# A wavelet block with attention on Trainium2: VectorE's order in the head, and where the last image's maps and attention layers stand

## The reference

```python
ll, lh, hl, hh = haar_dwt(x)                                  # 80 x 80 each
fused = relu(bn(conv1x1(concat(ll, lh, hl, hh), fusion_w)))   # 1024 -> 256 channels
sp_map = conv7x7(concat(mean_c(fused), max_c(fused)), sa_w)   # 2 -> 1 channel, 80 x 80
s = sigmoid(sp_map) * fused
ch = sigmoid(mlp(mean_hw(s)) + mlp(max_hw(s)))                # 256 -> 16 -> 256
proj = relu(bn(conv1x1(ch * s, proj_w)))                      # 256 -> 1024 channels
return haar_idwt(proj) + x
```

## Time and profile before

| | us |
|---|---|
| median of three runs | 2400.68 (2397.55 to 2400.82) |
| the profiled execution | 2394.07 |
| its span, first to last instruction | 2392.3 |

### The profile page before, as it was taken

One profiled execution on the slowest core, in us unless ns is written; L12 is line 12 of the kernel. 1 busy time (PEld: TensorE's weight loads), 2 busy tenths in 40 slices (PEclk: granted clock), 3 DMA queues, 4 the chain that ended last, 5 costly groups with the idle time before them and its releaser, 6 DMA issues. The chain is left out here.

```text
span 2392.3 us, 30200 instructions
## 1 busy us (share of the span) xinstructions
PE 2303.3 (96%) x11109; PEld 2039.9 (85%) x11109; DVE 2065.7 (86%) x2571; ACT 1137.2 (48%) x1535; POOL 584.9 (24%) x549
## 2 busy tenths in 40 slices
PE   7998799999999999999999999999999999998897
PEld 6886689888898988989899898988889898886786
DVE  6885688898888988899888989889888898889899
ACT  4443544465444554455444564446544464434433
POOL 0110122122221221211222112212212112133698
PEclk9999899999999999999999999999999999999999
DMA  5454499999999999999999999999999999989998
GB/s 188 168 183 147 151 277 283 278 310 284 294 286 295 288 286 288 288 281 306 282 277 297 293 307 281 283 278 297 295 293 283 283 307 280 280 238 286 346 354 324
DMA packets 112759, 660.54 MB, mean 276 GB/s; under 512 B 17698, under 2 KB 18788, under 8 KB 112356
## 3 DMA queue, kind: packets, MB, share of 16 engines
q1 hardware_dynamic: 84964, 479.04, 51.8%
q0 software_dynamic: 27648, 179.58, 39.2%
HBM read 448.24 MB, written 210.33 MB: 275 GB/s over the span
## 5 line engine op out<-in xcount | busy, mean ns | idle before, releaser
L542 PE MATMUL pp<-y_hi,wp_hi 128*128 128x480 f32 (+1 forms) x1792 | 670.5, 374 | 24.8 <-DVE sd L863 11.7
L633 ACT ACTIVATE x_hi<-xin 128x1920 fp32r<-128x1920 f32 (+1 forms) x224 | 418.7, 1869 | 542.9 <-PE pfs L570 461.0
L542 PE MATMUL pp<-y_lo,wp_hi 128*128 128x480 f32 (+1 forms) x1792 | 666.1, 372 | 0.0
L542 PE MATMUL pp<-y_hi,wp_lo 128*128 128x480 f32 (+1 forms) x1792 | 664.1, 371 | 0.0
L777 DVE TENSOR_TENSOR x_lo<-xin,x_hi 128x1920 fp32r<-128x1920 f32 (+1 forms) x224 | 461.5, 2060 | 214.1 <-ACT x_hi L633 213.1
L570 PE MATMUL pfs<-x_hi,wf_hi 128*128 128x480 f32 (+1 forms) x1648 | 616.4, 374 | 13.7 <-DVE x_lo L777 13.3
L570 PE MATMUL pfs<-x_lo,wf_hi 128*128 128x480 f32 (+1 forms) x1648 | 614.3, 373 | 0.0
L570 PE MATMUL pfs<-x_hi,wf_lo 128*128 128x480 f32 (+1 forms) x1648 | 614.2, 373 | 0.0
L666 ACT ACTIVATE relu<-pp,t 128x480 f32<-128x480 f32 (+1 forms) x448 | 285.6, 639 | 351.6 <-PE pp L542 351.2
L880 DVE SCALAR_TENSOR_TENSOR xre<-sd,both 128x960 f32<-128x960 f32 (+1 forms) x364 | 410.2, 1169 | 6.1
L542 PEld LDWEIGHTS pp<-y_hi,wp_hi 128*128 128x128 f32 x1792 | 338.2, 189 | 76.0 <-DVE sd L863 15.5
(11 more groups left out here) (105 smaller groups left out, 1595.5 us busy)
## 6 DMA issues: line engine op xcount, KB each, us to landing
xin<-in_x_dram SPq DMA_DIRECT2D x160, 960.0 KB, 7.8
out_dram<-xre SPq DMA_DIRECT2D x160, 960.0 KB, 7.5
xre<-in_x_dram POOLq DMA_DIRECT2D x136, 960.0 KB, 10.3
xin<-in_x_dram SPq DMA_DIRECT2D x64, 800.0 KB, 7.3
out_dram<-xre SPq DMA_DIRECT2D x63, 800.0 KB, 5.9
xre<-in_x_dram POOLq DMA_DIRECT2D x56, 800.0 KB, 9.5
xre<-in_x_dram SPq DMA_DIRECT2D x24, 960.0 KB, 7.0
sigb<-sig_scratch SPq DMA_DIRECT2D x28, 400.0 KB, 8.5
```

The lines of the kernel that those rows point to most:

```text
L542: mm = pe.matmul(pp[j][:, 0:n_px], w[:, kt, cols], y[:, s.pc, kt, 0:n_px], start=(kt == 0 and m == 0), stop=(kt == CT - 1 and m == 2))
L633: nc.scalar.activation(halves(x_hi, i, k), pairs(i, k), ACT.Copy).then_inc(xhi_ready[i], 1)
```

## The change

Four orders change, and no arithmetic.

- Head, VectorE (`head_body`, slots 0 to 20): `turn` comes first, then `x_lower` of the first half, then `pool_chunks`, both `gate`s, `spatial_maps`, `bands`, then `x_lower` of the second half. `turn` now stands ahead of the `x_lower` pair of its slot.
- Head, GpSimd: `channel_sum` no longer waits for the first half of `x_lo` of the next tile.
- Slot 112: TensorE's `gather` of the maps moves behind both halves of the projection, `spatial_maps` on VectorE behind the second `cells`, and `store_maps` on SyncE behind `store(s.kc, 0)` and `load_residual(s.kn, 1)`.
- Slot 118: the first attention layer stands between the banks LL and HH of the projection's second half, the second between HH and HL; ScalarE's relu of it stands ahead of the relu of HH; VectorE's `lower` of the next tile stands between the second `butterflies` and `cells` (before: at the top of slot 119).

```diff
             def body(s):
...
+                if s.phase == 0 and s.a:
+                    store_maps(s)
...
                 if s.c:
                     store(s.kc, 0)
                 if s.c_next and not adding(s.kn, 1):
                     load_residual(s.kn, 1)
+                if s.phase == 0 and not s.a:
+                    store_maps(s)
...
                 gp.wait_ge(f_ready, CT * (k + 1))
-                if s.load_next:
+                if s.load_next and s.c:
                     gp.wait_ge(xlo_ready[0], s.k + 2)
...
                 for n, j in enumerate((LH, LL, HH, HL)):
+                    if s.phase == LAST - 1 and not s.a and i == 1:
+                        if n == 2:
+                            squeeze_channels(s)
+                        if n == 3:
+                            excite_channels(s)
...
-                if s.phase == LAST and not s.a:
-                    excite_channels(s)
...
                 if s.c:
                     project(s, 1)
+                if s.phase == 0 and not s.a:
+                    gather(s)
...
                 for n, j in enumerate((LH, HH)):
+                    if n == 1 and i == 1 and s.phase == LAST - 1 and not s.a:
+                        hidden(s)
...
+            def head_body(s):
+
+                if s.turn:
+                    turn(s)
+                x_lower(s.k + 1, 0)
+                if s.phase == LAST - 1:
+                    pool_chunks(s)
+                if s.phase in GATED:
+                    for hand in range(2):
+                        gate(s, GATED[s.phase][hand])
+                if s.phase == 0:
+                    spatial_maps(s)
+                bands(s)
+                x_lower(s.k + 1, 1)
+                if s.c_next:
+                    lower(s.kn)
...
             def body(s):
-                ahead = s.phase == LAST
+                if not s.c:
+                    head_body(s)
+                    return
...
                 butterflies(s, 1)
+                if s.phase == LAST - 1 and not s.a:
+                    lower(s.kn)
                 cells(s, 1)
+                if s.phase == 0 and not s.a:
+                    spatial_maps(s)
```

More of the change, by code:

```diff
@@ L366, in load_sig, with store_maps @@
                              ).then_inc(sigb_landed[c % 2], 16)
+            def store_maps(s):
+                sp.wait_ge(across_ready, 2 * (s.nb + 1))
+                for m in range(2):
+                    sp.dma_start(map_dram[m:m + 1, :].rearrange("o (h p j) -> (o p) h j", h=2, j=GROUP),
+                                 across_all[:, m, :, :]).then_inc(map_stored, 16)
             def store_sig(s):
@@ L585, in convolve, with gather, squeeze_channels @@
                 mm.then_inc(conv_psum, 1)
+            def gather(s):
+                pe.wait_ge(mlp_ready, 2)
+                pe.wait_ge(blockmax_ready, s.k)
+                pe.wait_ge(blocksum_ready, s.k)
+                for to, blocks in ((across_sum, blocksum), (across, blockmax)):
+                    for h in range(2):
+                        n = NPX // GROUP // 2
+                        mm = pe.transpose(to[:, h * P:(h + 1) * P], blocks[:, h * n:(h + 1) * n], ident[:, :])
+                mm.then_inc(across_psum, 1)
+            def squeeze_channels(s):
+                pe.wait_ge(pool_ready, 2 * (s.nb + 1))
+                for i in range(CT):
+                    mm = pe.matmul(squeezed, squeeze[:, i, :], pool[:, i, :], start=(i == 0), stop=(i == CT - 1))
+                mm.then_inc(hid_psum, 1)
             def body(s):
@@ L614, in body @@
                     project(s, 1)
+                if s.phase == 0 and not s.a:
+                    gather(s)
                 if s.phase == 1 and not s.a:
                     convolve(s)
[L617 to L621, removed]
+                if s.phase == LAST - 1 and s.a:
+                    squeeze_channels(s)
             body(slots[0])
@@ L694, in upper, with hidden @@
                                          scale=ch[:, i:i + 1]).then_inc(hi_ready, 1)
+            def hidden(s):
+                act.wait_ge(hid_psum, s.nb + 1)
+                nc.scalar.activation(hid[:, :], squeezed, ACT.Relu, accum_out=hid_sum[:, :]).then_inc(hid_ready, 1)
             def body(s):
-                if s.phase == LAST:
-                    act.wait_ge(hid_psum, s.nb + 1)
-                    nc.scalar.activation(hid[:, :], squeezed, ACT.Relu, accum_out=hid_sum[:, :]).then_inc(hid_ready, 1)
+                if s.phase == LAST and s.a:
+                    hidden(s)
                 if s.phase == LAST:
@@ L950, in pool_chunks @@
                 nc.vector.tensor_reduce(pool[:, :, 1], part[:, 1, :, :], AX.X, ALU.max).then_inc(pool_ready, 1)
+            def head_body(s):
[13 more added lines that the diff above has]
+                    lower(s.kn)
             def body(s):
-                ahead = s.phase == LAST
+                if not s.c:
+                    head_body(s)
+                    return
                 if s.load_next:
                     x_lower(s.k + 1, 0)
[L956 to L966, removed]
+                butterflies(s, 0)
+                if s.phase == 0:
+                    turn(s)
+                if s.phase == LAST - 1:
+                    pool_chunks(s)
+                cells(s, 0)
                 if s.c_next and not s.next_is_first:
                     lower(s.kn)
-                if s.phase == LAST - 1 and not s.c:
-                    pool_chunks(s)
-                if s.turn and not (s.phase == 0 and s.c):
+                if s.turn and s.phase != 0:
                     turn(s)
@@ L974, in body @@
                     gate(s, GATED[s.phase][0])
-                if s.load_next and other(s.k) == other(s.k + 1):
+                if s.load_next:
                     x_lower(s.k + 1, 1)
-                if s.phase == 0:
+                if s.phase == 0 and s.a:
                     spatial_maps(s)
@@ L980, in body @@
                     lower(s.kn)
[L981 to L984, removed]
+                butterflies(s, 1)
+                if s.phase == LAST - 1 and not s.a:
+                    lower(s.kn)
+                cells(s, 1)
+                if s.phase == 0 and not s.a:
+                    spatial_maps(s)
                 if s.phase in GATED:
```

## The result

The change took 33.7 us off the median: 2365.39 us (2359.91 to 2370.51, four runs) against 2399.11 for the kernel before on the same chip, a ratio of 0.9861 with an interval of 0.9835 to 0.9887. Two more comparisons of the same file gave 0.9888 (0.9873 to 0.9902) and 0.9865 (0.9844 to 0.9887). The profiled execution took 2366.2 us, with a span of 2364.4; the prediction had 2368.6 for that and 2375 for the median. It was right in direction and in range, and 9.6 us high.

The account below looks back on a forecast made before the run. VectorE's order was taken to hold up TensorE in the head, engines other than TensorE to bind the tail. Head -28, slot 112 +2.5, slot 118 0 sum to -25.5: 2368.6 profiled, 2375 median after carrying over 6.6; range 2364 to 2387.

Parts of the forecast that it names:

- slots 1 to 13: Head: the new VectorE order leaves 3.5 of TensorE's 7.6 us idle; gain 4, bounds 7 and a loss of 6.
- slots 14 and 15: Head: TensorE's 7.1 us wait for blockmax goes, and 1 us of slow clock with it; gain 8.
- slots 16 to 20: Head: VectorE becomes the bound at 12 us a long slot against TensorE's 10.7; gain 13.5, bounds 9 and 17.
- slot 21: End of the head: runs at full clock without a long idle ahead of it; gain 2.5.
- the exclusion: Head: GpSimd's sum and a two-input VectorE instruction can't overlap; 1.0 us charged per turn, about 5 us more gain without it.
- The wait for the broadcast: Slot 16: gate 0's broadcast lands at 11.1 us after the convolution's end, where VectorE would come at 9.7.
- Tail, slot 112: Map stores queue behind three transfers, so the convolution starts 1.7 us later; loss 2.5, bounds -1 (a gain) and 5.
- a convolution that starts earlier relative to the middle's end: Tail: sign that the forecast is wrong and the tail gains.
- the 2147 less the head's gain: Tail, slot 112: sign that the forecast is right, SyncE's map stores issued after this time.
- Tail, slot 118: TensorE starts slot 119 2 us earlier, but GpSimd's adding waits for a residual's DMA; 0, bounds gain 2.5, loss 1.
- (2): Rival: the tail pays as TensorE's waits suggest, 5.3 us for the gather and 2 for the gate; 2365, chance 0.1.
- (3) to (5): Rivals: port and DMA cost double in head, 2390, chance 0.11; slower turns, 2411, 0.02; no effect, 2400, 0.03.

Follow-up runs that it names:

- sum_small: The full change with GpSimd's channel sum in slots 1 to 20 cut to 8 columns; ratio 0.9839 to the kernel before, 2358.4 us.
- gate_only: The kernel before with the change of slot 118 alone; ratio 1.0001 (0.9992 to 1.0010).
- maps_only: The kernel before with the change of slot 112 alone; ratio 1.0005 (0.9993 to 1.0017).
- head_order: The full change, but outside slots 14 and 15 turn stands behind bands or gates and GpSimd's sum waits for x_lo again; ratio 0.9870 to the kernel before.

## Why the prediction was right, and where its sizes were off

By slot starts in the two traces, the terms of the head:

```
                     before   after   gain   forecast
slots 1 to 13        139.5    134.1    5.4     4
slots 14 and 15       32.1     23.8    8.3     8
slots 16 to 20        72.1     56.8   15.3    13.5
slot 21*              13.7     11.3    2.3     2.5
to its projection    289.7    258.1   31.5    28
```

(*: to its projection. The last row is counted from the span's start, the terms from slot 1.)

**Slots 1 to 13.** The mechanism was as told: the sum meets `x_lo`, `turn` pays 1.0 us, TensorE's waits stay under 1 us (three, 0.74 to 0.85, all at a tile of 400 columns or behind one). The longer ones, up to 1.7, are in slots 17 to 20. The remaining idle was 2.5 us by the window, where 3.5 was reckoned. The sentence that without the exclusion the head would gain 5 us more had the size too small and the place half wrong: `sum_small` shows 6.6, of which only 2.8 here and 4.0 in slots 16 to 20, where VectorE is the bound and the sum's microsecond had been reckoned in the slot's 12.0 without being called a cost of the exclusion.

**Slots 14 and 15** came out as forecast, with no idle before the gather.

**Slots 16 to 20.** Slots 17 to 20 take 12.2, 11.4, 11.2 and 11.5 us. The wait for the broadcast that was forecast as new is 0.83 us:

```profile
200.54 0.99 DVE L918 CUSTOM_DVE_ANT_0 fused<-fused,sigb 128x800 f32<-128x800 f32 x1 [0.83 <-DMA sigb<-sig_scratch]
```

It was reckoned at 1.4 (11.1 less 9.7). Slots 17 to 19 cost VectorE's sum, 34.8 us for the 34.6 reckoned (12.0 and twice 11.3). Two things made the gain larger than forecast. The 1 us taken off for shared DMA engines wasn't paid, and the last step, `turn` and the first `x_lo` of slot 20, took 4.9 us instead of 6.1: the sum met the `x_lo` ahead of it, and the maximum took 0.56. The bounds, 9 and 17, held it.

**Tail, slot 112.** Right in mechanism: SyncE's order and not TensorE sets the convolution, the map load falls from 4.9 to 1.7 us, the stores behind the transfers cost more than that, and TensorE idles 5.2 to 10 us (8 to 9 forecast) and then runs at the lower clock. Two signs named beforehand were misleading: a convolution that starts earlier relative to the middle's end was to show a gain, and in the first trace it did start 2 us earlier, through one quicker DMA; for the same reason the maps' stores were issued at 2112.80, some 3 us before the 2147 less the head's gain that was to show the forecast right. Over seven traces the edit is at +1.8 to +2.3 us. What of this reaches the end isn't settled; the time is 1.2 us with an interval from -1.7 to 4.1.

**Tail, slot 118.** Zero was right and for the reason given: `gate_only` is 1.0001, and GpSimd's run still begins on a DMA, behind a wait of 6.5 us. TensorE's start of slot 119 comes 1.3 us earlier, where 2 was reckoned: it is 7.4 us behind TensorE's last wait for `sd` in `gate_only` and 8.7 in `before`.

**The sum.** The profiled execution missed by 2.4 us (2366.2 for 2368.6). The other 7.2 us of the median's miss come of the step that carried over 6.6 us from one profiled execution to the median: after's own profiled execution lies 0.8 *above* its median. Before's trace was a quick one: from the last fusion to the end it took 271.8 us, the least of all seven in the table, whose others take 274.0 to 281.5. Between medians the gain is 33.7, 27.0 (2397.1 less 2370.1) and 30.3 us (2398.9 less 2368.6) in three comparisons, around the 31.5 of the head, against a forecast sum of 25.5.

**The rivals.** (2), the tail paying 7.3 us as TensorE's waits suggest, gives 2365, which is the time measured, but by chance, and it is wrong all the same: `maps_only` and `gate_only` exclude 7.3. (3) to (5) are out by the time.

## What to carry to other kernels

When an engine with slack is late, look at the order of its queue before its work: moving what nobody waits for into the gap ahead of an input that isn't ready took 31 us out of a head of 290 without removing an instruction. An idle engine in a stretch where another (here VectorE, GpSimd and the DMA engines) sets the end is no sum to be gained; four edits there moved waits from one place to another and nothing at the end that the intervals show. Where two engines exclude each other, ask before moving one which instruction of the other will pay instead, and whether that engine has time to spare there: `bands` paid what the maximum no longer did and it cost nothing in slots 1 to 13, while the gates paid in slots 16 to 18, where VectorE is the bound, and nothing was won.

## What the runs showed of the hardware

A GpSimd sum of 8 columns still took 0.99 us on average, against 1.94 for 480 columns in the changed kernel and 1.33 in `head_order`, and yet it left VectorE's maximum at 0.635 us. Mostly it is released in the midst of `x_lo` and ends with it: in one slot it ran from 116.61 to 117.69, and `x_lo` from 115.47 to 117.63. So a short GpSimd instruction costs VectorE nothing here, however long its row in the profile. Where a full sum met `x_lo`, the maximum, a gate or an instruction of `bands`, that one VectorE instruction lost 0.85 to 1.04 us, however short it was: 1.32 us instead of 0.29 for an 80 x 80 one. Two reductions beside a sum lost nothing, in the one case that a trace shows. And in a tail whose DMA engines are busy to 0.99, one accumulating DMA of the same size landed after 7.6 us in one trace and 12.3 in another, which moved the convolution more than the edit of slot 112 did (1.8 to 2.3).
